# Attention, normalisation moved into the step that makes the values, and what follows one step earlier

## What is computed

```
x   = x + tanh(g_x) * Attention(layernorm(x), ctx, ctx, mask)      # 16 heads of 8, rope on q and k, bias everywhere
n   = layernorm(x)
idx = argmax(n @ Wr + br);  gate = softmax(n @ Wr + br)[idx]       # 8 experts, one per row
out = x + tanh(g_f) * gate * (gelu(n @ W1[idx] + b1[idx]) @ W2[idx] + b2[idx])
```

## Time and profile before

| | us |
|---|---|
| median of 3 runs (304.95, 305.37, 306.65) | 305.37 |
| the profiled execution, its own time | 306.31 |
| its span, first to last instruction | 304.5 |
| PE busy in the span | 244.9 (80%) |
| DVE busy | 191.4 (63%) |
| POOL busy | 181.8 (60%) |
| ACT busy | 166.4 (55%) |

### The profile page before, as it was taken

One profiled execution on the slowest core, in us unless ns is written; L12 is line 12 of the kernel. 1 busy time (PEld: TensorE's weight loads), 2 busy tenths in 40 slices (PEclk: granted clock), 3 DMA queues, 4 the chain that ended last, 5 costly groups with the idle time before them and its releaser, 6 DMA issues.

```text
span 304.5 us, 10523 instructions
## 1 busy us (share of the span) xinstructions
PE 244.9 (80%) x3529; PEld 210.9 (69%) x3529; DVE 191.4 (63%) x639; ACT 166.4 (55%) x481; POOL 181.8 (60%) x222
## 2 busy tenths in 40 slices
PE   1458799997998878888889868869568999999960
PEld 1246687786787766777768656758458899999960
DVE  5546777988798799977797784645623443334420
ACT  2155688886787775778678661342503344444410
POOL 7466567567478875688968764056463455544450
PEclk9999999997999999999999995897787999999995
DMA  7711465464344734152422213310323322100100
GB/s 222 213 17 31 99 199 137 98 174 122 94 140 112 194 68 127 20 151 39 145 44 44 43 39 94 80 41 33 93 87 96 106 67 62 51 29 30 37 19 0
DMA packets 58535, 26.63 MB, mean 87 GB/s; under 512 B 38608, under 2 KB 53989, under 8 KB 58484
## 3 DMA queue, kind: packets, MB, share of 16 engines
q1 hardware_dynamic: 55204, 20.15, 26.9%
q0 software_dynamic: 2272, 4.46, 4.4%
q10 hardware_dynamic: 1008, 1.35, 1.5%
HBM read 16.70 MB, written 5.51 MB: 73 GB/s over the span
## 4 chain that ended last, share of the span: by engine, by line
PE 39%; DVE 13%; issue 13%; POOL 12%; SPq 7%; ACT 6%; DMA 4%; another core or an unknown queue 4%; POOLq 1%; DVEq 0%; ACTq 0%
PE ps L745 11%; SPq L406 5%; PE ps L788 4%; PE ps L729 3%; POOL rot L545 3%; POOL rot L539 3%; PE ps L803 2%; POOL rot_s L541 2%; PE ps L727 2%; PE ps L728 2%; DMA kbd<-kT 2%; DVE mx L1210 2%; PE ps L778 2%; PE ps L830 2%
## 5 line engine op out<-in xcount | busy, mean ns | idle before, releaser
L560 POOL DMA_INDIRECT out<-fin,got x39 | 37.8, 970 | 40.5 <-DVE fin L1259 28.5
L1210 DVE TENSOR_REDUCE mx<-ps 128x16 f16<-128x1024 f32 x32 | 39.1, 1222 | 18.5 <-PE ps L803 14.5
L745 PE MATMUL ps<-w_f,hT 128*128 x312 | 47.5, 298 | 0.0
L512 POOL DMA_INDIRECT rows<-x_all,dest_i x32 | 33.2, 1037 | 21.9 <-DVE x_all L1060 14.7
L1259 DVE SCALAR_TENSOR_TENSOR fin<-ps,got 128x128 f32<-128x128 f32 x39 | 13.7, 350 | 49.2 <-PE ps L745 34.6
L745 PEld LDWEIGHTS ps<-w_f,hT 128*128 128x128 f32 x312 | 40.2, 202 | 1.2 <-issue 0.2
L788 PE MATMUL ps<-vx,pr 128*64 128x32 f32 x1024 | 37.6, 228 | 4.1 <-ACT pr L589 1.7
L788 PEld LDWEIGHTS ps<-vx,pr 128*64 128x64 f32 x1024 | 34.1, 143 | 8.0 <-issue 2.8
L589 ACT ACTIVATE pr<-ps 128x1024 f32<-128x1024 f32 x32 | 32.7, 1022 | 9.4 <-PE ps L830 9.0
L539 POOL TENSOR_TENSOR rot<-qk,cf 128x256 f32<-128x256 f32 x32 | 23.4, 732 | 22.6 <-ACT qk L609 16.0
L657 ACT ACTIVATE hT<-ps 128x512 f32<-128x512 f32 x39 | 23.3, 597 | 22.6 <-PE ps L729 15.3
(11 more groups left out here) (156 smaller groups left out, 606.9 us busy)
## 6 DMA issues: line engine op xcount, KB each, us to landing
kbd<-kT SPq DMA_DIRECT2D x128, 32.0 KB
got<-rows SPq DMA_DIRECT2D x39, 72.0 KB
w_f<-in_W_rows SPq DMA_DIRECT2D x8, 256.0 KB, 2.9
w_r<-in_W_last_row SPq DMA_DIRECT2D x8, 256.0 KB, 3.3
w_f<-in_L_ffn_W SPq DMA_DIRECT2D x8, 256.0 KB, 5.0
x_all<-in_x SPq DMA_DIRECT2D x3, 512.0 KB, 4.9
xt_all<-in_x_t SPq DMA_DIRECT2D x3, 512.0 KB, 4.4
ct_all<-in_ctx SPq DMA_DIRECT2D x3, 512.0 KB, 4.3
```

Of the source, the lines that this page charges most:

```text
L512: pool.indirect_dma_start(out=rows, out_offset=bass.IndirectOffsetOnAxis(ap=dest_i[:, t:t + 1], axis=0), in_=x_all[:, t, :], in_offset=Non ...
L560: pool.indirect_dma_start(out=out_d, out_offset=bass.IndirectOffsetOnAxis(ap=got_i[:, u % GOT, R_ID:R_ID + 1], axis=0), in_=fin[:, u % FRI ...
L745: mm = pe.matmul(o, hT[:, par, c, :], w2_f[:, bass.ds(e, 1), c, :].rearrange("p o n -> p (o n)"), start=False, stop=(c == FC - 1))
L1210: dve.tensor_reduce(mx[:, t % 2, 0:H], ps_s[:, :].rearrange("p (h k) -> p h k", k=S), AX.X, ALU.max).then_inc(mx_done, 1)
```

## The change

Values of tile t are normalised in step t+4 rather than t+5, and on DVE this stands directly ahead of the reduction L1210 rather than at the start of the step. PE's transpose and output projection, ACT's copy, DVE's sum with x and its statistics, the routing of each group and the list of scatters all move to one step earlier. The small matmul that makes the output bias moves ahead of the first transpose within step 4, and its split (`output_bias_halves`) with it. On PE the expert number of tile u is evaluated into a register after the output projection in step F0 + u, and the wait for DVE ahead of the second layer stays only for u < 6 and the last tile. Nothing is computed differently.

```diff
         def out_step(u):
-            return F0 + 5 + u // 2 if u < 3 else min(max(SCATTER_AT) - 2 + u, STEPS - 1)
+            return F0 + 4 + u if u < 2 else min(max(SCATTER_AT) - 1 + u, STEPS - 1)
-        GROUP_AT = {b - 1 + 6: g for g, (a, b) in enumerate(GROUPS)}
+        GROUP_AT = {b - 1 + 5: g for g, (a, b) in enumerate(GROUPS)}
-        SCATTER_AT = {**{i: 1 for i in (*range(15, 21), *range(22, 32))}, 32: 4, 36: 3, 37: 2, 38: 2, 41: 3, 42: 2}
+        SCATTER_AT = {**{i: 1 for i in (*range(14, 20), *range(21, 32))}, 32: 3, 35: 3, 36: 2, 37: 2, 40: 3, 41: 2}
@@ ACT @@
-                t = i - 5
+                t = i - 4
                 if live(t):
                     act.wait_ge(onT_done, t + 1)
@@ PE @@
-                experts[u] = (words[v // PACK] >> (3 * (v % PACK))) & 7
+                experts[u] = pe.snap((words[v // PACK] >> (3 * (v % PACK))) & 7)
...
             def rows_transposed(u):
-                expert_numbers(u)
...
             def second_layer(u):
                 pe.wait_ge(f_gelu, u + 1)
-                wait(pe, f_fin, used(y_bank, u))
+                if u < 6 or u == NS - 1:
+                    wait(pe, f_fin, used(y_bank, u))
...
+                if i == 4:
+                    pe.wait_ge(s_prep, 5)
+                    pe.wait_ge(s_wow, 2)
+                    pe.wait_ge(s_idw, 1)
+                    pe.matmul(bank[4][:, P:P + QX], c_bc[:, :], id_wr[:, :], start=True, stop=True).then_inc(s_c, 1)
-                t = i - 5
+                t = i - 4
                 if live(t):
                     pe.wait_ge(on_done, t + 1)
...
-                t = i - 5
+                t = i - 4
                 if live(t):
                     pe.wait_ge(onT_ev, t + 1)
                     pe.matmul(ps_op, pick, c_h[:, :], start=True, stop=False)
                     pe.matmul(ps_op, onT[:, t % 2, :], wo_x[:, :], start=False, stop=True).then_inc(op_done, 1)
+                if tile(i - F0):
+                    expert_numbers(i - F0)
                 if tile(i - F0 - 2):
                     second_layer(i - F0 - 2)
@@ DVE @@
-                t = i - 5
-                if live(t):
-                    dve.wait_ge(pv_done, t + 1)
...
...
-                t = i - 6
+                t = i - 5
                 if live(t):
                     dve.wait_ge(op_done, t + 1)
...
+                if i == 4:
+                    output_bias_halves()
+                t = i - 4
+                if live(t):
+                    dve.wait_ge(pv_done, t + 1)
+                    wait(dve, on_done, t - 1)
+                    o_ps = ps_o.rearrange("p (h c) -> p h c", c=16)
+                    dve.reciprocal(rden[:, t % 2, :], o_ps[:, :, HD]).then_inc(rden_done, 1)
+                    dve.wait_ge(rden_done, t + 1)
+                    wait(dve, onT_done, t - 1)
+                    dve.tensor_tensor(on[:, t % 2, :].rearrange("p (h d) -> p h d", d=HD), o_ps[:, :, 0:HD],
+                                      rden[:, t % 2, :].rearrange("p (h o) -> p h o", o=1).broadcast_to([P, H, HD]),
+                                      ALU.mult).then_inc(on_done, 1)
                 t = i - 2
                 if live(t):
                     dve.wait_ge(s_done, t + 1)
```

More of the change, by code:

```diff
@@ L834, in step @@
                 if i - 2 in GROUP_AT:
-                    if live(i - 5):
-                        pe.wait_ge(onT_ev, i - 4)
+                    if live(i - 4):
+                        pe.wait_ge(onT_ev, i - 3)
                     else:
@@ L839, in step @@
                     rank_of(GROUP_AT[i - 2])
-                t = i - 5
+                t = i - 4
                 if live(t):
+                    if t == 0:
+                        pe.wait_ge(s_cs, 2)
                     pe.wait_ge(onT_ev, t + 1)
@@ L852, in step @@
                     pe.transpose(ps_mx, mx[:, t % 2, :], ident_h).then_inc(mxT_done, 1)
-                if i == 4:
-                    pe.wait_ge(s_prep, 5)
-                    pe.wait_ge(s_wow, 2)
-                    pe.wait_ge(s_idw, 1)
-                    pe.matmul(bank[4][:, P:P + QX], c_bc[:, :], id_wr[:, :], start=True, stop=True).then_inc(s_c, 1)
             pipeline(step)
@@ L1136, in step @@
                                       ).then_inc(f_lo, 1)
-                t = i - 5
-                if live(t):
-                    dve.wait_ge(pv_done, t + 1)
-                    wait(dve, on_done, t - 1)
-                    o_ps = ps_o.rearrange("p (h c) -> p h c", c=16)
-                    dve.reciprocal(rden[:, t % 2, :], o_ps[:, :, HD]).then_inc(rden_done, 1)
-                    dve.wait_ge(rden_done, t + 1)
-                    wait(dve, onT_done, t - 1)
-                    dve.tensor_tensor(on[:, t % 2, :].rearrange("p (h d) -> p h d", d=HD), o_ps[:, :, 0:HD],
-                                      rden[:, t % 2, :].rearrange("p (h o) -> p h o", o=1).broadcast_to([P, H, HD]),
-                                      ALU.mult).then_inc(on_done, 1)
                 t = i
```

4 lines of the change are left out of this document (removed).

## The result

The changed kernel takes 314.49 us (median of 4 runs, 313.63 to 316.44) against 305.90 for the kernel before: ratio 1.0267, 95% interval 1.0194 to 1.0341. The profiled execution took 313.63 us, its span is 311.8 us against 304.5. The forecast was 303.2 us in a range of 297.5 to 309.5: wrong in sign, and outside the range. Medians are of all runs; the ratios leave out executions that took over 1.5% longer than the fastest of their kernel, so that a ratio can differ a little from the quotient of two medians.

What follows compares the result with a forecast made beforehand. It took a loop of waits (DVE's list in some steps) to bound attention, then a tail with holes, then busy PE. Terms summed to -2.2 us: 304.1 us profiled, 303.2 us median, range 297.5 to 309.5.

Steps and rivals of the forecast that it cites:

- a tail shorter by 3 us or more: Sign for the sum: stretch from 178.6 to 231 us must shorten this much, or the sum is wrong.
- Normalisation ahead of the maxima, common steps: Attention: maxima start 0.05 us later in some twelve steps, PE's 0.3 us push hidden by L778's wait for POOL; +0.7 us.
- The same in DVE-bound steps: Eleven routing and weight steps: normalisation enters DVE's late stretch, +4.4, and PE's next projection comes later, +1.4; together +5.8 us.
- The sign that I had given for it: Period of attention steps 13 to 15, 19, 20, 27 and 28 should rise by 0.5 to 0.7 us.
- DVE becomes the bound of attention: Slower rival, DVE's list between L1155 and L1210: some 14 steps pay 0.69 us each, sum +4.4, 309.8 us; chance 0.28.
- Step 4: Attention step 4: bias matmul, split and first normalisation in a row ahead of the maxima; +0.5 us, bounds 0 and 1.
- POOL's two powers: Step 11: L490 and L498 no longer back to back, step 12 loses less, step 31 pays 0.9; -0.9 us.
- Tail of attention: End of attention: last tile leaves PE in step 35 instead of 36; -2.5 us, bounds 0 and -3.4.
- bursts: POOL's runs of indirect transfers: two runs one transfer shorter; -2.5 us, bounds 0 and -6.9.
- loads of expert words: Expert part: loads move from ahead of the transpose to behind the first layer; -0.3 us, bounds 0 and -1.2.
- Expert steps: PE's queue: without wait L94 the hole before L743 closes, -0.10 us in some 30 steps; -3.0 us, bounds 0 and -4.8.
- The rival that the queue gains nothing: Expert steps: extra register operation or array floor at 1.95 us makes the term 0, sum +0.8, 306.2 us; chance 0.19.

Runs made afterwards that it cites:

- kernel 3: Changed kernel with PE's transpose of the normalised values behind the score block and the output projection in the next step; 311.86 us, ratio 1.0156.
- kernel 4: kernel 1 with only VectorE's half of the move: reciprocal and normalisation of tile i-4 ahead of the maxima; 309.42 us, ratio 1.0105.
- kernel 1: Kernel before with only the expert part: expert number in a register, no second-layer wait from tile 6 on except the last; 304.90 us, ratio 0.9926.
- kernel 5: Changed kernel with the sum with x and second statistics of tile i-5 ahead of the scaled q on VectorE; 288.89 us, ratio 0.9847.
- kernel 14: kernel 4 with the sum with x and second statistics of tile i-6 ahead of the scaled q on VectorE; 303.90 us, ratio 0.9924.
- kernel 8: Changed kernel with routing, sends of rows and returns of tiles in their steps of before; 303.53 us, ratio 1.0364.
- kernel 17: kernel 15 with POOL's power for tiles 16 to 19 in step 12 instead of step 11; 299.14 us, ratio 0.9775.
- kernel 18: Expert part alone (as kernel 1) with POOL's power for tiles 16 to 19 in step 12 instead of step 11; 302.61 us, ratio 0.9885.
- kernel 2: Changed kernel with reciprocal and normalisation moved on VectorE ahead of the routing operations, right behind the second bn_aggr; 315.20 us, ratio 1.0275.
- kernel 10: kernel 5's edit plus step 4's bias matmul behind its projections and the bias halves behind the scaled q, on the changed kernel; 304.91 us, ratio 0.9957.
- kernel 13: Kernel before with the expert part alone, a repeat of kernel 1 in another call; 303.89 us, ratio 0.9936.
- kernel 15: kernel 1 with the sum with x and second statistics ahead of the scaled q only in steps with routing work; 302.90 us, ratio 0.9888.

## Why the prediction was wrong

For the profiled execution the sum said -2.2 and the span grew by 7.3 us. Three places make the difference of 9.5: attention (+8.55 in place of +5.6), step 4 (+2.96 in place of +0.5 up to step 5), and the stretch from qk of tile 31 to z of tile 10 (-1.2 in place of -5.3). The last is the largest by size, and by the prediction's own sign, a tail shorter by 3 us or more, it makes the sum wrong. But with that stretch as forecast the kernel would still have been slower; what no term had was the closed loop.

**Normalisation ahead of the maxima, common steps (+0.7): the step that failed.** It said that TensorE's transpose "has to wait for the product" and pushes the rest of the step by 0.3 us, and that this "is hidden by the 0.54 us that L778 waits for POOL". The cover was not there. What is pushed is not only the end of TensorE's step but the score block, exp and the copy of mxT, and L778 waits for that copy too. Plain steps grew by 0.31 to 0.33 us. That this is the 0.3 of the prediction is in part luck: its 0.3 was a delay within one step, the measured one is the difference between the period before and a loop of seven links. With the transpose behind the block (kernel 3) plain steps fell to 4.92 us. A delay inside a loop cannot be set against a wait on the same loop before it is known what else that wait's owner is waiting for. In size: the seven steps that are plain in both kernels (8, 14, 16, 17, 28 to 30) take 2.4 us more, and all that VectorE's half and step 12 don't explain is 4.7 us (8.55, less the 5.50 of kernel 4, plus the 1.63 by which kernel 1's attention is shorter than before), against +0.7.

**The same in DVE-bound steps (+5.8).** Right: the 0.49 us left a place where VectorE waits anyway and came to stand where it is late. Kernel 4 against kernel 1 shows it (+5.5 us net, fourteen steps longer), and kernels 5 and 14 show that work put into the empty stretch brings it back. The sign that I had given for it, steps 13 to 15, 19, 20, 27 and 28 longer by 0.5 to 0.7, didn't come in the changed kernel (20 and 27 are shorter, 13 longer by 1.1), since the groups' work moved to the step ahead. The rival "DVE becomes the bound of attention" had this mechanism, the number of steps (some 14) and the direction; it put attention's part at +9.7 +0.7 -0.9 = +9.5, nearer to the 8.55 than my +5.6, and was to decide over 7 us. Its 309.8 us still fall short, by step 4 and the tail. I gave it 0.28 where the rows, traced once round the loop, would have carried more.

**Step 4 (+0.5).** Mis-sized: +2.95. TensorE waited 1.33 us for on, then ran at half the clock (the matmuls of the score block follow each other by 0.11 us instead of 0.06 in the timeline). By kernel 8, with the same wait and the full clock, some 1.5 us of it are the clock, and the order itself costs the other 1.4.

**POOL's two powers (-0.9).** The mechanism holds: kernels 17 and 18 give the price of the coincidence in step 12, 0.6 us where the clock holds (6.15 to 5.59) and 4.25 us (9.39 to 5.14) where it falls. But the changed kernel's own gain in step 12, 7.70 to 6.07 us, doesn't prove it: kernel 1 leaves the powers together and takes 6.15. Most of what the earlier trace rows cost was not the wait but the slower clock behind it: 7.70 us at a granted clock of 0.67 from 72 us on, 6.15 in kernel 1 at 1.00, 5.59 without the coincidence.

**Tail of attention (-2.5), bursts (-2.5), loads of expert words (-0.3).** From qk of tile 31 to the first z the changed kernel takes 15.83 us against 17.29: -1.5 for the tail. Even that is not sure to be the earlier tail: the granted clock there was 1.00 against 0.70, and kernels 2, 3 and 10, which have the earlier tail too, take 18.38, 16.68 and 16.99. From the first z to that of tile 10 it takes 38.91 against 38.65, so the bursts gave nothing. Results that came late did not become fewer, seven waits and 26.9 us against seven and 27.6 (189 to 245 us; they answer to the earlier trace rows):

```profile
DVE fin L1261 <- remote: 7.6, 2, 5.7
...
ACT hT L657 <- remote: 7.0, 1, 7.0
...
DVE x_all L1161 <- remote: 3.8, 1, 3.8
...
DVE rden L1204 <- remote: 3.3, 1, 3.3
```

I had counted transfers in a row; the late results moved to other instructions with them. Kernel 8, in a call without such waits, does show 3 to 4 us for the earlier routing, so the term exists where they don't. Why it is lost where they do stays open.

**Expert steps (-3.0).** Right in mechanism, a little large. The -3.4 of the table holds luck: 1.1 us of it is the one step from z of tile 10 to z of tile 11, 2.90 us at a granted clock of 0.67 before and 1.78 at 1.00 after. From z of tile 11 to z of tile 38 the changed kernel takes 51.31 us against 53.59, kernels 1 and 13 51.10 and 51.39: -2.2 to -2.5. The rival that the queue gains nothing is refuted. The Trainium skill (Perfetto Trace Analysis, Identifying Dependency Chains) on EventSemaphore instructions put ahead of one with several waits agrees once more: with one wait left, TensorE's queue holds none ahead of L743.

## What to carry to other kernels

Before an operation is moved to an earlier place in an in-order list, look at what stood around it: if it filled the wait for another engine, the old place stays empty after the move and the new one pays the full length (0.31 to 0.53 us in fourteen steps of kernel 4), unless something whose input is ready is put into the hole. Follow a delay once round the loop until it comes back to its own instruction, and take a wait as cover only if nothing else on that loop feeds the waiting instruction. And price a wait of TensorE with the clock that may come after it: two POOL operations set a step apart were worth 0.6 us in kernel 18 and 4.25 us in kernel 17, and the difference is the clock behind the wait.

## What the hardware showed beyond that

**A call without the late results.** In the call with kernels 5 to 8 the kernel before took 292.36 us; in all others 305.9 to 307.1. As far as the profiles show, the difference lies behind attention. Kernel 5 there, and kernel 10 (the same with the bias edit, 16.99, 39.19 and 53.18 us long) in another call, in windows of qk of tile 31, z of tile 0, z of tile 10, z of tile 38:

```profile
174.01:189.11 15.10, 11.39 (x179) 9.44 (x174) 10.56 (x38) 6.58 (x19) 7.27 (x8) 0.77 0.26 58
189.11:216.04 26.93, 21.54 (x298) 19.19 (x296) 16.87 (x77) 13.85 (x27) 17.42 (x18) 1.00 0.31 92
```

```profile
174.94:191.93 16.99, 10.21 (x179) 8.27 (x174) 10.45 (x38) 6.58 (x19) 7.26 (x8) 0.90 0.29 64
191.93:231.12 39.19, 28.34 (x298) 25.64 (x296) 16.90 (x77) 13.74 (x27) 18.80 (x19) 0.78 0.25 74
```

The same instructions, and the second window 12.3 us apart; 6.8 us of that is TensorE's busy time for the same 298 matmuls, at a granted clock of 0.78 against 1.00. The waits for "remote" are absent from all four profiles of that call. What delays the results elsewhere, while POOL's indirect transfers run in a row, stays open. That it goes with the chip is not shown: the record has the same chip number for this call and for that of kernels 17 and 18, where the kernel before took 306.35 us. It is a reason to compare only within one call.

**POOL slows VectorE's small operations.** A scaling of 128x56 values takes 0.18 us alone and 1.19 us in step 18, started 0.31 us into a POOL operation and ended 0.08 us behind the next one (POOL L539 from 111.78, L541 to 113.20). A tensor_reduce of the same size (L1011, at 161.08) takes 0.21 us in the midst of POOL's L541 (160.93 to 161.65). The Trainium skill (SBUF — State Buffer, Who interferes with whom) says that a VectorE instruction with two SBUF inputs contends with a GpSimd instruction that reads SBUF, and that tensor_reduce never does; the trace agrees with both. In the routing operations of attention VectorE's busy time differs by 4.3 us (16.1 against 11.8 in kernel 5), which I had not looked for.

**The clock after a wait.** TensorE ran at a granted clock of 0.50 to 0.51 after waits of 2.03 us (step 12 of kernel 15) and 2.12 us (step 25 of the changed kernel), yet at 1.00 after one of 2.35 us in step 18. Waits of one length went either way: 1.33 and 1.32 us in step 4 (0.55 in the changed kernel, 1.00 in kernel 8), and 1.67 us ahead of L778 in step 12 (0.67 in the kernel before, 1.00 in kernels 1 and 13). So the length of the wait alone doesn't decide. The window behind the wait of step 25:

```profile
155.42:158.17 2.75, 2.75 (x30) 2.61 (x30) 1.47 (x3) 0.81 (x2) 1.03 (x2) 0.50 0.64 190
```

What else decides was not tried.
